# Attention loop: TensorE's order within a step is difference, turning, first component, values, second component

## What is computed

```
q1, q2, k1, k2 : per head 8 features each;  v : per head 16
L1 = l2norm(q1) @ l2norm(k1).T * cos_scale
L2 = l2norm(q2) @ l2norm(k2).T * cos_scale
G  = tanh(delta_gain * (L1 - L2))
A1 = softmax(L1 + G);  A2 = softmax(L2 - G)
y  = (A1 - lambda_full * A2) @ v
y  = y * rsqrt(mean(y*y) + RMS_EPS) * subln_weight * (1 - LAMBDA_INIT)
return y @ Wo.T + bo
```

## Time and profile before

| | us |
|---|---|
| median of 3 runs | 797.56 (795.8 to 797.76) |
| profiled execution, its own time | 796.23 |
| its span, first to last instruction | 794.0 |
| TensorE matmul busy | 660.3 (83%) |
| VectorE busy | 564.8 (71%) |
| ScalarE busy | 485.4 (61%) |
| GpSimdE busy | 228.4 (29%) |
| mean granted TensorE clock | 0.976 |

### The profile page before, as it was taken

The page is one execution under the profiler, slowest core; times in us unless marked ns, Lnnn a source line. Parts: engine busy times, 40 slices in busy tenths (PEclk is TensorE's granted clock), DMA queues, the critical chain, the costliest instruction groups (busy, mean ns, idle before and its releaser), DMA issues.

```text
span 794.0 us, 9725 instructions
## 1 busy us (share of the span) xinstructions
PE 660.3 (83%) x3476; PEld 282.5 (36%) x3514; DVE 564.8 (71%) x1087; ACT 485.4 (61%) x468; POOL 228.4 (29%) x359
## 2 busy tenths in 40 slices
PE   4999899999999478887878788778787787979796
PEld 2576545454544112222221122122222111456364
DVE  5656321407161688888999889999988999768756
ACT  1344323233334359999999999889899989422311
POOL 3601100101014475312434513743933002011001
PEclk9999999999999679999999999999999999999998
DMA  8000200000000110011100111010110013300250
GB/s 296 1 1 1 82 1 0 1 0 1 0 1 0 27 27 14 14 28 28 27 14 19 23 27 28 15 25 15 28 27 14 14 27 107 107 1 14 62 165 27
DMA packets 16752, 26.00 MB, mean 33 GB/s; under 512 B 2496, under 2 KB 7360, under 8 KB 16320
## 3 DMA queue, kind: packets, MB, share of 16 engines
q1 hardware_dynamic: 16704, 25.38, 11.6%
HBM read 15.87 MB, written 1.11 MB: 21 GB/s over the span
## 4 chain that ended last, share of the span: by engine, by line
PE 50%; DVE 30%; ACT 11%; issue 7%; DMA 1%; POOL 0%; SPq 0%; POOLq 0%; ACTq 0%; DVEq 0%
DVE hid L1115 10%; DVE hid L1112 9%; PE ps L512 7%; PE ps L522 7%; ACT probs L821 7%; PE ps L600 6%; PE ps L593 5%; PE ps L612 4%; PE ps L499 3%; ACT w_hh L851 3%; PE ps L621 3%; PE ps L532 2%; PE ps L419 2%; PE ps L450 2%; PE ps L545 2%
## 5 line engine op out<-in xcount | busy, mean ns | idle before, releaser
L851 ACT ACTIVATE w_hh<-hid 128x2048 f32<-128x2048 f32 x128 | 243.8, 1905 | 12.0 <-DVE hid L1115 12.0
L593 PE MATMUL ps<-q_s,k_s 128*128 128x512 bf16 (+1 forms) x474 | 163.4, 394 | 32.4 <-DVE hid L1112 22.2
L1112 DVE TENSOR_TENSOR hid<-ps,probs 128x1024 f32<-128x1024 f32 x128 | 156.3, 1221 | 37.2 <-ACT probs L821 35.9
L821 ACT ACTIVATE probs<-ps,gain 128x1024 f32<-128x1024 f32 x128 | 142.2, 1111 | 40.2 <-PE ps L593 37.0
L1115 DVE SCALAR_TENSOR_TENSOR hid<-ps,probs 128x1024 f32<-128x1024 f32 x128 | 155.4, 1214 | 0.0
L600 PE MATMUL ps<-w_hh,v_h 128*32 128x512 f32 x1024 | 139.4, 617 | 5.4 <-issue 4.4
L593 PE MATMUL ps<-q_w,k_w 64*128 64x512 bf16 x256 | 97.8, 396 | 54.6 <-DVE hid L1115 53.0
L593 PEld LDWEIGHTS ps<-q_s,k_s 128*128 128x128 bf16 (+1 forms) x512 | 42.0, 96 | 148.0 <-DVE hid L1112 60.4
L1449 POOL TENSOR_SCALAR rs<-mv 128x4 f32<-128x4 f32 x32 | 7.4, 231 | 256.5 <-DVE mv L930 256.4
L1023 DVE SCALAR_TENSOR_TENSOR hid<-ps,s_b,rot 128x512 f32<-128x512 f32 x16 | 11.9, 750 | 87.1 <-ACT rot L794 87.1
L877 ACT ACTIVATE u_q<-ps 128x512 f32<-128x512 f32 x32 | 19.1, 598 | 67.8 <-PE ps L612 67.7
(11 more groups left out here) (249 smaller groups left out, 923.3 us busy)
## 6 DMA issues: line engine op xcount, KB each, us to landing
k_w<-k_s SPq DMA_DIRECT2D x32, 128.0 KB, 2.3
q_w<-q_s SPq DMA_DIRECT2D x32, 128.0 KB, 2.3
w_hh<-w_rows SPq DMA_DIRECT2D x4, 1024.0 KB, 10.6
w_hh<-in_b_h SPq DMA_DIRECT2D x2, 1024.0 KB, 8.6
hid<-w_rows SPq DMA_DIRECT2D x2, 1024.0 KB, 6.2
part<-w_rows SPq DMA_DIRECT2D x8, 256.0 KB, 7.3
x_res<-in_x SPq DMA_DIRECT2D x4, 256.0 KB, 6.1
tab<-in_rope SPq DMA_DIRECT2D x1, 1024.0 KB, 7.0
```

The costliest lines, as they stand in the source:

```text
L593: last = mm(ps[:, base + half, :], k_op[rows, u, keys], q_op[rows, u, half * CHUNK:(half + 1) * CHUNK], start=True, stop=True)
L821: A(gg[:, mt % 2, :], banks[:, 0:2 * CHUNK], ACT.Tanh, scale=gain[:, u:u + 1]).then_inc(S["g"], 1)
L851: A(ee[:, mt % 2, :], zz[:, mt % 2, :], ACT.Exp).then_inc(S["e"], 1)
L1112: v.tensor_tensor(zz[:, mt % 2, 0:SEQ], banks[:, 2 * CHUNK:4 * CHUNK], gg[:, mt % 2, :], ALU.add).then_inc(S["z1"], 1)
```

## The change

`c_scores` is split into `c_diff`, `c_first` and `c_second`, and the order in a step becomes: difference of s + 2, turning, first component of s + 2, values of s, second component of s + 2. Every matmul stays, with the same waits on the same signals. The lists of ScalarE, VectorE, GpSimdE and SyncE hold the same instructions in the same order.

```diff
-            def c_scores(s, u, mt):
+            def c_product(s, u, mt, base, halves):
                 keys = slice(mt * P, (mt + 1) * P)
...
+            def c_diff(s, u, mt):
+                pe.wait_ge(S["g"], s)
+                c_product(s, u, mt, 0, ((every, k_s, q_s), (every, k_s, q_s))).then_inc(S["dd"], 1)
+            def c_first(s, u, mt):
+                pe.wait_ge(S["z1"], s)
+                c_product(s, u, mt, 2, ((low, k_s, q_s), (high, k_w, q_w))).then_inc(S["l1"], 1)
+            def c_second(s, u, mt):
+                pe.wait_ge(S["z2"], s)
+                c_product(s, u, mt, 4, ((low, k_w, q_w), (high, k_s, q_s))).then_inc(S["l2"], 1)
...
-                    if mt < BT - 2:
-                        c_scores(s + 2, u, mt + 2)
-                    elif n < NH - 1:
-                        if mt == BT - 2:
-                            pe.wait_ge(S["turn_read"], turns_done(("q", n + 1)))
-                            pe.wait_ge(S["crossed"], 64 * (n + 2))
-                        c_scores(s + 2, 1 - u, mt + 2 - BT)
+                    if later:
+                        if mt2 == 0:
+                            pe.wait_ge(S["turn_read"], turns_done(("q", n2)))
+                            pe.wait_ge(S["crossed"], 64 * (n2 + 1))
+                        c_diff(s + 2, n2 % 2, mt2)
+                    use = turning(n, mt)
+                    if use:
+                        c_turning(use)
+                    if later:
+                        c_first(s + 2, n2 % 2, mt2)
                     elif mt == BT - 1:
                         pe.wait_ge(S["g"], NH * BT)
                         d_up(0)
                     if mt == 0:
                         pe.wait_ge(S["vh"], n + 1)
                         pe.wait_ge(S["accout"], n)
-                    c_values(s, u, mt)
-                    use = turning(n, mt)
-                    if use:
-                        c_turning(use)
+                    c_values(s, n % 2, mt)
+                    if later:
+                        c_second(s + 2, n2 % 2, mt2)
```

More of the change, by code:

```diff
@@ L582, in router @@
                 return last
-            def c_scores(s, u, mt):
+            every, low, high = slice(0, P), slice(0, P // 2), slice(P // 2, P)
+            def c_product(s, u, mt, base, halves):
                 keys = slice(mt * P, (mt + 1) * P)
[L586 to L595, removed]
+                for half, (rows, k_op, q_op) in enumerate(halves):
+                    last = mm(ps[:, base + half, :], k_op[rows, u, keys],
+                              q_op[rows, u, half * CHUNK:(half + 1) * CHUNK], start=True, stop=True)
+                return last
+            def c_diff(s, u, mt):
[7 more added lines that the diff above has]
+                c_product(s, u, mt, 4, ((low, k_w, q_w), (high, k_s, q_s))).then_inc(S["l2"], 1)
             def c_values(s, u, mt):
@@ L659, in _ @@
             pe.wait_ge(S["crossed"], 64)
-            c_scores(0, 0, 0)
-            c_scores(1, 0, 1)
+            for mt in range(2):
+                c_diff(mt, 0, mt)
+                c_first(mt, 0, mt)
+                c_second(mt, 0, mt)
             for n in range(NH):
-                u = n % 2
                 for mt in range(BT):
                     s = n * BT + mt
-                    if mt < BT - 2:
-                        c_scores(s + 2, u, mt + 2)
-                    elif n < NH - 1:
-                        if mt == BT - 2:
-                            pe.wait_ge(S["turn_read"], turns_done(("q", n + 1)))
-                            pe.wait_ge(S["crossed"], 64 * (n + 2))
-                        c_scores(s + 2, 1 - u, mt + 2 - BT)
+                    later = s + 2 < NH * BT
+                    n2, mt2 = divmod(s + 2, BT)
+                    if later:
[8 more added lines that the diff above has]
+                        c_first(s + 2, n2 % 2, mt2)
                     elif mt == BT - 1:
```

## The result

| | before | after |
|---|---|---|
| median, us | 797.66 (7 runs, 795.8 to 798.01) | 800.49 (7 runs, 799.0 to 803.09) |
| profiled execution, its own time | 796.23 | 800.04 |
| its span | 794.0 | 797.9 |
| mean granted TensorE clock | 0.976 | 0.969 |

The ratio of after to before is 1.0045, with a 95% interval of 1.0028 to 1.0063. The time lies within the stated range (793.0 to 802.5). The likeliest case, no change, didn't come: the kernel became slower, and the whole interval lies above 1, its lower end just under the 0.3% (1.003) that the prediction set as the limit of no change.

A forecast was written before the change was run, and what follows sets the result against it. ScalarE was taken to bound the loop. Profiled 796.23 us - 10.2 gain + 10.4 loss = 796.4, or 797.8 at the median: no change, own range 795.2 to 800, 8-in-10 range 793.0 to 802.5.

The forecast's parts named there:

- The likeliest case, no change: Whole kernel: gain and loss nearly cancel, 797.8 us, own range 795.2 to 800; chance 0.47.
- What bounds the kernel: Attention loop: ScalarE bounds it, tanh following tanh after 2.81 us, so a head can't be shorter than 22.5 us.
- Ordinary heads: Heads outside 10 to 12: most tanh waits for TensorE go; heads 1 to 3 23.0 us each; gain together 10.2 us.
- The fear that slow values would delay the second component: Head 0: at TensorE's lower clock values take 1.94 us, delaying the second component; gain taken as 0.8, bounds 0 and 2.5.
- The chain's mechanism and its period: Heads 10 to 12, turnings in successive steps: twelve wait for VectorE's bank copy, queueing work; period 4.1 us, 4.7 for projections.
- the loss of heads 10 to 12, 10.4 us: Heads 10 to 12: turnings waiting for the bank cost 5.1 + 5.1 + 0.2 = 10.4 us; bounds 7 and 14.
- slower by the clock: Rival, heads with successive turnings: TensorE idles, its clock falls, six hits of about 1.0 us, +6, 803.5 us; chance 0.14.
- a granted clock of 1.00 in heads 10 and 12: Sign of being right in the new profile: TensorE's granted clock stays at 1.00 in both heads.
- Heads 13 to 15: Last three heads: routing on VectorE leaves a gain of 0.4 us, bounds 0 and 1.5.
- Slower by VectorE: Rival, ordinary heads: VectorE's 21 of 22.5 us unevenly spread, half the gain lost, +4.5, 802 us; chance 0.14.
- Faster: Rival: chained waits cost 7 instead of 10.4 us and head 0 gives 2, -4.6, 793 us; chance 0.25.
- The change doesn't do what it says: Rival: holds only if the turnings didn't wait for the bank; no size or chance given.

The follow-up runs named there:

- e5_best: Changed kernel, but second component ahead of the values, and the twelve turnings directly following a step with one put last, behind the values: 783.76 us, ratio 0.9833.
- e6_acc_first: Changed kernel, but VectorE copies the accumulator ahead of both additions of a head's second step instead of behind them: 801.27 us, ratio 1.0054.
- e9_mixed: As e5_best, but in head 0 and heads 10 to 12 the values stand ahead of the second component: 782.12 us, ratio 0.9816.
- e8_again: The changed kernel run once more, unaltered: 801.81 us, ratio 1.0068.
- e7_fill_both: Changed kernel, but in the twelve chained steps TensorE computes both components once more ahead of the turning, results overwritten: 798.62 us, ratio 1.0022.
- e2_fill: Changed kernel, but in the twelve chained steps TensorE computes the second component once more ahead of the turning, result overwritten: 801.0 us, ratio 1.0053.
- e1_close_last: Changed kernel, but the twelve turnings directly following another step with one stand last, behind the second component: 784.92 us, ratio 0.9855.
- e10_chain_head10: As e1_close_last, but only in heads 11 and 12; head 10 keeps the changed order, chain and all: 790.47 us, ratio 0.9924.
- e4_values_only: Changed kernel, but the turning goes back to the end of the step; values stay ahead of the second component: 790.03 us, ratio 0.9919.
- e3_turn_only: Changed kernel, but the second component goes back ahead of the values; the turning stays behind the difference: 794.37 us, ratio 0.9972.

## Why the prediction was right, and where it wasn't

**What bounds the kernel: right.** ScalarE's 2.81 us per step (22.5 per head) is the floor, which e5_best nearly reaches with 22.66 us per head.

**Ordinary heads: right, a little low.** 23.0 us was worked out and 22.98 measured, with the single wait of 0.45 at the fourth tanh, and e6_acc_first confirmed its cause. Heads 0 to 9 gained 255.1 - 244.3 = 10.8 us against 9.8. The missing 1.0 is head 0: it gained 2.0 instead of 0.8. The fear that slow values would delay the second component there wasn't borne out; e5_best and e9_mixed point the other way, since head 0 is 1.8 us shorter with the values first. Part of that is the clock: the eight executions with head 0 in the order of after or e9_mixed lasted 31.15 to 32.01 us there, and e8_again, whose second low stretch of the clock in head 0 is as long as that of e5_best (6.8 us), took 32.01 against 32.94. By that one pair the order is worth some 0.9, and the rest may be where the clock fell. The 1.0 us taken off for VectorE's work in heads 4, 5, 6 and 8 was about right (measured for heads 4 to 9: 4.2, predicted 4.3).

**The chain's mechanism and its period: right.** The periods were 4.2 us against 4.1, and 4.71 against 4.7 for the first projection (4.47 for the second, and 4.64 and 4.37 for the router's two); the turning waits for the copy as said. (Its carried starts 544.2 to 552.6 are up to 0.2 us off what its own two periods give, which changes nothing in the end.) Where no fall disturbed it, head 10 grew by 31.63 - 26.19 = 5.4 us (e8_again, e7_fill_both) and head 12 by 30.34 - 24.84 = 5.5 (e2_fill, whose added product doesn't lengthen the chain: its turnings at 525.36 and 530.08 us stand 4.72 apart, as in e8_again), predicted 5.1 each. Head 11 was to grow by 0.2; without a fall it lasted 25.92 in e6_acc_first (whose edit touches only the accumulator's copy), +0.15.

**The step that failed: the loss of heads 10 to 12, 10.4 us, was costed at full clock alone.** It measured 14.9. Of that, 5.4 + 5.5 + 0.15 = 11.1 is the chain as worked out; the rest, some 3.9, is the clock: head 10 32.93 - 31.63 = 1.3 for one fall, head 12 32.39 - 30.34 = 2.05 for two, head 11 26.42 - 25.92 = 0.5 for one. With the chain alone the sum would have been 11.1 - 10.8 = +0.3 us, plus the 0.3 of heads 13 to 15, less the 0.5 at the two ends of the loop: the forecast of no change. So it is the rival "slower by the clock" that turned no change into slower. It was put at +6 us and a chance of 0.14, from six hits of 1.0 us (797.8 + 6 is 803.8, where it wrote 803.5); there were four of 0.5 to 1.3 us, 1.0 in the mean. Its price per hit was good and its chance too small: the rows against it were of the wrong kind. It had also named a granted clock of 1.00 in heads 10 and 12 as a sign of being right, and that sign failed. The mechanism was only half foreseen: it tied the clock to the chained waits alone, but two of the four falls (519.5 and 553.7 us, 1.8 of the 3.9) stand where kernels without chained waits but with the values first fell as well. The prediction argued that a chained period holds 2.7 us of work in 4.1 and that the clock had stayed at 1.00 through a stretch with 1.70 of 3.4 us busy. After the change it fell behind stretches with 1.33 busy, but also with 2.02 and 2.27, and it stayed up behind one with 2.01. In these rows the busy time ahead doesn't tell a fall from none; one row in which the clock held was no evidence against twelve new idle places.

The Trainium skill (TensorE: Matmul & The Clock Gate, A second HAM failure mode: psum-queue depth-cycling) describes a clock that goes back and forth when TensorE idles briefly and often between groups of matmuls that cycle through PSUM banks. This case agrees more than the prediction allowed: one fall in the loop behind 295 us before, five after, four of them in heads 10 to 12, where TensorE's waits ahead of the chained turnings of head 10 are 1.13 to 2.07 us. It doesn't say which idle brings a fall, and neither do these runs.

**Heads 13 to 15: wrong sign.** Predicted 0.4 us shorter, they became 0.3 longer; e8_again has 76.64, 0.6 shorter, with no fall in them. The profile of after has one at 662.9 us, and that of before one at 636.3. Within this, the sign depends on where a fall lands.

**The other rivals.** "Slower by VectorE" (half of the ordinary gain lost) fell with the 22.98 us. "Faster" needed the chain to cost 7 us; it cost 11.1. "The change doesn't do what it says" fell with the first added wait.

**A sum of two terms that cancel.** Gain and loss were both good to about 1 us, and their difference is 0.3 at full clock. The prediction said so, and its own range of 795.2 to 800 for no change holds the forecast at full clock, but not the measured 800.49.

## What to carry to other kernels

Before moving work ahead in an engine's list, look for the places where what it waits for is only just being made: there it holds back everything behind it. Treating just those places (twelve of the loop's 59 turnings) differently turned +0.45% into -1.45%. Gains of two edits that remove the same waits overlap, while their losses need not (9.7 and 0.4 us apart, 14.9 together), and where a change puts short idles into TensorE's list, price its clock in the main sum and not as an unlikely rival: here it was a quarter of the loss and nearly all of the slowdown.

## What the runs showed of the hardware that I had not expected

The granted clock fell to 0.50 for 3.4 us at a time in heads in which TensorE is busy most of the time. Head 10 of after as one window:

```profile
512.10:545.00 32.90, 24.18 (x158) 7.95 (x156) 24.53 (x32) 23.03 (x18) 12.37 (x21) 0.95 0.08 17
```

TensorE was busy 24.18 of 32.90 us there, with no single idle above 2.07 us in its timeline from 515 to 537, and still had a fall; one fall cost 0.5 to 2.0 us in heads 10 to 12. Where it falls varies between executions of one kernel: at 519.5, 553.7, 591.2, 601.5 and 662.9 us in one of after, at 393.2, 502.4, 553.6, 570.7 and 594.6 in the other. But some places recur. One is early in head 10, at 518.1 to 521.2 us in after, e1_close_last, e2_fill, e6_acc_first, e9_mixed and e10_chain_head10 and at 526.1 in e4_values_only, where TensorE comes out of a wait of 1.5 to 2.8 us; in e8_again the same wait of 2.07 us stood there, and the clock stayed up. Another is head 9 at 498.9 to 502.4 us, in seven of the twelve executions, those of e3_turn_only, e5_best and e1_close_last among them, so neither half of the change is its condition. What decides between a fall and none stays open.
